# Graph attention and two-expert routing on one core: narrower rows for the first list, centred gate logits from raw rows, and a new order of the steps around them

## The reference

```python
# x: 64 x 128 x 128 (graphs g, nodes n, features d), adj: 64 x 128 x 128 of 0/1
h = layernorm(x)                                  # no scale, no bias
Wh = h @ W.T;  e = leaky_relu(Wh@a1 [:,None] + Wh@a2 [None,:], 0.2)
x = x + softmax(where(adj > 0, e, -9e15)) @ Wh    # the attention layer
z = layernorm(x)
logits = z @ gate_w + gate_b                      # 16 experts
top 2 of softmax(logits), renormalised -> gates
x = x + sum over the 2 chosen e of gate_e * ((silu(z @ w1[e]) * (z @ w2[e])) @ w3[e])
```

## Time and profile before

| | us |
|---|---|
| median of 3 runs (518.23 to 519.63) | 519.61 |
| the profiled execution | 513.99 |
| its span, first to last instruction | 512.2 |
| PE busy / DVE busy | 393.6 / 250.7 |
| ACT busy / POOL busy | 224.2 / 257.1 |

### The profile page before, as it was taken

The page is one execution under the profiler, slowest core; times in us unless marked ns, Lnnn a source line. Parts: engine busy times, 40 slices in busy tenths (PEclk is TensorE's granted clock), DMA queues, the critical chain, the costliest instruction groups (busy, mean ns, idle before and its releaser), DMA issues.

```text
span 512.2 us, 11503 instructions
## 1 busy us (share of the span) xinstructions
PE 393.6 (77%) x2993; PEld 357.2 (70%) x2994; DVE 250.7 (49%) x978; ACT 224.2 (44%) x583; POOL 257.1 (50%) x284
## 2 busy tenths in 40 slices
PE   6889788867685867079988788852998887888890
PEld 3678677755564766079977788852998887888880
DVE  4788989865786453024433344340342523424250
ACT  2799576563574513024424344320443423525240
POOL 5222346775328666426554655561355554555554
PEclk9999999987887678569999999985899999999996
DMA  3544345646173356577666666424654664555500
GB/s 105 158 130 135 90 154 158 185 155 208 43 228 116 135 178 235 204 236 248 222 221 193 202 215 225 152 71 124 184 182 158 189 186 160 164 179 187 164 28 1
DMA packets 75547, 83.35 MB, mean 163 GB/s; under 512 B 10564, under 2 KB 60111, under 8 KB 75504
## 3 DMA queue, kind: packets, MB, share of 16 engines
q1 hardware_dynamic: 66032, 61.58, 39.7%
q0 software_dynamic: 9472, 21.26, 11.8%
HBM read 36.06 MB, written 28.94 MB: 127 GB/s over the span
## 4 chain that ended last, share of the span: by engine, by line
PE 47%; issue 18%; DVE 10%; SPq 7%; POOL 6%; DMA 4%; ACT 3%; another core or an unknown queue 2%; ACTq 1%; POOLq 0%; DVEq 0%
PE bank L499 26%; PE bank L512 11%; PE bank L371 5%; SPq L303 4%; POOL sorted_rows L1014 3%; POOL rstd L1005 2%; DMA shared<-in_adj_dram 2%; DVE prob L931 1%; DMA R<-sorted_rows 1%; DVE stats L688 1%; SPq L318 1%; DVE h L698 1%; DVE R L744 1%; PE bank L419 1%
## 5 line engine op out<-in xcount | busy, mean ns | idle before, releaser
L499 PE MATMUL bank<-xT,w_t 128*128 128x128 f32 x1280 | 181.9, 285 | 25.2 <-issue 16.4
L499 PEld LDWEIGHTS bank<-xT,w_t 128*128 128x128 f32 x1280 | 164.1, 199 | 30.1 <-issue 19.7
L632 ACT ACTIVATE hT<-bank 128x256 f32<-128x256 f32 x160 | 60.5, 384 | 171.2 <-PE bank L499 97.1
L931 DVE TENSOR_TENSOR prob<-hT,bank 128x256 f32<-128x256 f32 x160 | 67.2, 420 | 136.9 <-ACT hT L632 76.9
L1039 POOL DMA_INDIRECT out_dram<-R x80 | 78.3, 979 | 80.1 <-DVE R L940 51.1
L512 PE MATMUL bank<-W,prob 128*128 x640 | 102.5, 284 | 14.3 <-issue 10.0
L1039 POOL DMA_INDIRECT sorted_rows<-R x80 | 78.4, 980 | 69.5 <-DVE R L940 48.3
L512 PEld LDWEIGHTS bank<-W,prob 128*128 128x128 f32 x640 | 86.8, 196 | 19.5 <-issue 18.6
L940 DVE SCALAR_TENSOR_TENSOR R<-bank,R 128x128 f32<-128x128 f32 x160 | 55.1, 346 | 65.9 <-PE bank L512 56.5
L1014 POOL DMA_INDIRECT sorted_rows<-R,ROW x64 | 62.7, 979 | 29.5 <-issue 16.7
L371 PE MATMUL bank<-ident,R 128*128 128x128 f32 x224 | 39.1, 299 | 45.7 <-DMA R<-sorted_rows 26.5
(11 more groups left out here) (129 smaller groups left out, 382.4 us busy)
## 6 DMA issues: line engine op xcount, KB each, us to landing
R<-sorted_rows SPq DMA_DIRECT2D x160, 130.0 KB
w_t<-W SPq DMA_DIRECT2D x80, 256.0 KB
W<-in_L_ffn_w_dram SPq DMA_DIRECT2D x48, 128.0 KB
sorted_rows<-pad SPq DMA_DIRECT2D x34, 130.0 KB
R<-in_x_dram SPq DMA_DIRECT2D x16, 256.0 KB
shared<-in_adj_dram SPq DMA_DIRECT2D x16, 256.0 KB
sorted_rows<-R POOLq DMA_INDIRECT x80
out_dram<-R POOLq DMA_INDIRECT x80
```

The lines of the kernel that those rows point to most:

```text
L499: ins = nc.tensor.matmul(H[k][:, m * P:(m + 1) * P], w_t[:, par, k, m * P:(m + 1) * P], xT[:, par, k * P:(k + 1) * P], start=True, stop=True)
L632: nc.scalar.activation(sil[:, k, :], H[k][:, 0:HC * P], ACT.Silu).then_inc(silu_ready, 1)
L931: V.tensor_tensor(hidT[:, k, :], sil[:, k, :], H[k][:, HC * P:2 * HC * P], ALU.mult).then_inc(hid_ready, 1)
```

## The change

1. The row kept for list 0 is 128 raw values of x2, two row numbers, two gates, mean and inverse root: 134 floats, 536 bytes. The normalised values aren't stored in it. DVE normalises a quad's rows once they are loaded (`normalize_rows`), two tiles after each of the first two `gate_hidden` of the quad before. Rows of list 1 keep 1,040 bytes and their normalised half. The row slots are a buffer of their own.
2. Gate logits are computed from raw x2: PE turns x2, multiplies by a centred `gate_w` (`centre` is the identity minus 1/128), DVE multiplies by the inverse root and then adds the bias. ACT's second normalisation goes, and so does round 20: step 4 is now part of step 3, and every later step of a batch is one round earlier.
3. ACT normalises two graphs of each group for the attention (`BY_ACT`), DVE the other two.
4. DVE, PE and ACT have new orders in a round (DVE: first aggregate and epsilon ahead of the x2 sum; PE: turn of x2 first, gate logits and attention behind the turn of h).
5. Experts: rows are turned after the third `up` of a quad (`TURN`), in both lists; quad 3 is finished before the rows of quad 4 are turned; the 16 padding blocks of list 1 stand behind the rows and weights of quads 6 and 7 (eight each); PE does 30 bf16 matmuls of 512 columns between the lists (`SWITCH`).

```diff
-    ROW2, DEST, GATE = 2 * D, 2 * D + 1, 2 * D + 2
+    ROW2, DEST, GATE = D, D + 1, D + 2
+    MEAN = GATE + NL
+    RSTD = MEAN + 1
+    WIDTH = (RSTD + 1, D + MEAN)
...
-        rows = R[:, 0:RB * QT, :]
+        rows = sb("rows", [P, RB * QT, D + RSTD + 1])
...
-            for i in range(NI + 4):
-                steps = {k: 0 <= i - k < NI for k in range(-1, 5)}
+            for i in range(NI + 3):
+                steps = {k: 0 <= i - k < NI for k in range(-1, 4)}
...
+        def early(c, q, behind):
+            return c == 0 and isinstance(q, int) and q == NQA + behind
+        def carried(row, c):
+            return row[:, D:D + WIDTH[0]] if c == 0 else row[:, 0:WIDTH[1]]
...
             load_up(3, 1)
-            for b in range(NE // QT):
-                clear_pads(1, b * QT, pad_in[1])
...
             for q in (RB, RB + 1):
                 load_quad(0, q, q - RB, 1)
                 load_up(q, q % 2)
+                for b in range(NE // QT // 2):
+                    clear_pads(1, ((q - RB) * (NE // QT // 2) + b) * QT, pad_in[1])
...
+                if has(3):
+                    pe.wait_ge(x2_ready, k + 1)
+                    turn(TH2, lambda g: R[:, k * GG + g, 0:D], x2_turned)
                 if has(2):
                     turn(TP, lambda g: prob[:, par, g * N:(g + 1) * N], prob_turned)
+                if chosen is not None:
+                    count(chosen)
+                if has(0):
+                    turn(TH, lambda g: h[:, par, g * D:(g + 1) * D], h_turned)
+                if has(3):
+                    for g in range(GG):
+                        ins = nc.tensor.matmul(LO[:, g * NE:(g + 1) * NE], x2T[:, g * N:(g + 1) * N], gw_c[:],
+                                               start=True, stop=True)
                 if has(2):
                     for g in range(GG):
                         ins = nc.tensor.matmul(HP[:, g * D:(g + 1) * D], probT[:, g * N:(g + 1) * N],
                                                Wh[:, par, g * D:(g + 1) * D], start=True, stop=True)
...
+                if c == 0:
+                    pe.wait_ge(h2_ready, q * QT + QT)
+                else:
+                    pe.wait_ge(xs_in[slot], (nth + uses(slot) + 1) * (16 * QT))
...
+                if c:
+                    pe.wait_ge(xT_ready, NQ)
+                    keep_warm(SWITCH, XP)
...
-                        if k == 0 and not last:
+                        if k == TURN and not last and not early(c, q, -1):
                             turn_rows(c, q + 1, (at + 1) % RB, nth + (at + 1) // RB)
...
-                    if last:
+                    if last or early(c, q, -1):
                         for k in range(QT - LAG, QT):
                             down(c, q, at, k, e[k])
+                    if early(c, q, -1):
+                        turn_rows(c, q + 1, (at + 1) % RB, nth + (at + 1) // RB)
...
+                for g in range(BY_ACT):
+                    nc.scalar.activation(h[:, par, g * D:(g + 1) * D], R[:, i * GG + g, 0:D], ACT.Identity,
+                                         bias=shift[:, par, g:g + 1], scale=rstd[:, par, g:g + 1])
...
+                    V.tensor_tensor(logits, LO[:, 0:GG * NE].rearrange("p (g e) -> p g e", e=NE),
+                                    R[:, k * GG:(k + 1) * GG, RSTD:RSTD + 1].broadcast_to([P, GG, NE]),
+                                    ALU.mult).then_inc(logits_scaled, 1)
...
+            def normalize_rows(q, at, nth, tiles):
+                slot = at % RB
+                dve.wait_ge(xs_in[slot], (nth + 1) * (16 * QT))
+                for k in tiles:
+                    r = rows[:, slot * QT + k, :]
+                    V.tensor_scalar(r[:, 0:D], r[:, D:2 * D], r[:, D + MEAN:D + MEAN + 1], r[:, D + RSTD:D + RSTD + 1],
+                                    ALU.subtract, ALU.mult).then_inc(h2_ready, 1)
...
+                        if c == 0 and k < 2 and not last and not early(c, q, -1):
+                            normalize_rows(q + 1, at + 1, nth + (at + 1) // RB, range(2 * k, 2 * k + 2))
...
-            DISPATCHED = {8: 4, 9: 4, 10: 4, 11: 6, 12: 6, 13: 5, 14: 3, 15: 3, 16: 4}
+            DISPATCHED = {7: 4, 8: 4, 9: 4, 10: 6, 11: 6, 12: 5, 13: 3, 14: 3, 15: 5, 16: 3}
```

More of the change, by code:

```diff
@@ L60, in gat_moe_kernel @@
     NOWHERE = 2 * XROWS
-    xs = [nc.dram_tensor(f"sorted_rows{c}", (XROWS, DW), F32, kind="Internal").ap() for c in range(NL)]
+    xs = [nc.dram_tensor(f"sorted_rows{c}", (XROWS, WIDTH[c]), F32, kind="Internal").ap() for c in range(NL)]
     ctx = ExitStack()
@@ L358, in _, with keep_warm @@
             pe.wait_ge(const_steps, 7)
-            for _ in range(WARM):
-                nc.tensor.matmul(RT[:], ones_bf[:], ones_bf[:, 0:1].broadcast_to([P, GG * N]), start=True, stop=True)
+            def keep_warm(n, into):
+                for _ in range(n):
+                    nc.tensor.matmul(into[:], ones_bf[:], ones_bf[:, 0:1].broadcast_to([P, GG * N]), start=True, stop=True)
+            keep_warm(WARM, RT)
             pe.wait_ge(small_in, 80)
-            pe.wait_ge(const_steps, 12)
+            pe.wait_ge(const_steps, 13)
             pe.wait_ge(setup_v, 1)
@@ L431, in iteration @@
                 if i == 0:
[L432 removed]
+                    nc.tensor.matmul(RT[:], ident[:], x2T[:], start=True, stop=True)
             def choose(b):
@@ L553, in iteration @@
                     nc.scalar.activation(probT[:], TP[:], ACT.Copy).then_inc(probT_ready, 1)
-                if has(3):
-                    k = i - 3
-                    act.wait_ge(shift_ready, k + 1)
-                    for g in range(GG):
-                        row = R[:, bass.ds(k * GG + g, 1), :].rearrange("p a d -> p (a d)")
-                        ins = nc.scalar.activation(row[:, 0:D], row[:, D:2 * D], ACT.Identity,
-                                                   bias=shift[:, 1 - par, g:g + 1],
-                                                   scale=rstd[:, 1 - par, GG + g:GG + g + 1])
-                    ins.then_inc(h2_ready, 1)
                 if chosen is not None:
@@ L657, in quad @@
                         silu(q * QT + (c * NT + k), k)
-                        if k == 0 and not last:
+                        if k == (QT - 1 if early(c, q, -1) else TURN) and not last:
                             copy_rows(c, q + 1, 1 - par)
@@ L950, in quad @@
                                     table=q if c == 0 and isinstance(q, int) and q in (1, 2) and k == LAG else None)
-                        elif not first:
+                        elif not first and not early(c, q, 0):
                             add_row(c, t + (k - LAG), at + RB - 1, k + (QT - LAG))
```

243 lines of the change are left out of this document (136 added, 107 removed).

## The result

The changed kernel took 534.38 us (median of 6 runs, 527.12 to 537.89) where the kernel before took 519.62 on the same chip: a ratio of 1.025, 95% interval 1.019 to 1.031. It is slower, and 34 us over the forecast.

A forecast was written before the change was run, and what follows sets the result against it. PE, ACT and DVE nearly fill the attention stage, PE bounds the lists, with a 59.6 us hole between. Terms -27 (to quad 4), +5, +7, 0, -3.5, and -1 for the dispatch, give -19.5 from 519.61: 500 us, range 494 to 507.

The forecast's parts named there:

- A: Attention rounds: DVE loses 0.33 us a round, PE's work unchanged; 15 rounds give -5 us, bounds 0 and -8.
- B: End of the attention stage: one round less before the last choice, -4 us, bounds -1 and -7.
- PE holds it: Attention rounds: one case for the bound of 0, in which PE keeps the round from getting shorter.
- C: From last choice to quad 4: -18 us; first tile of quad 4 near 201 instead of 228.18.
- C's two bounds: List 0's 16 padding blocks before quad 4: 16.5 us if issue sets the pace, 8.5 if bytes do.
- E: List 0: PE's turn waits 0.6 us a quad for DVE's normalisation; +7 us, bounds 0 and 12.
- D: List 0: list 1's padding behind quads 6 and 7 uses up SP's lead; +5 us, bounds 0 and +12.
- rival 3: List 0: VectorE becomes its pace, PE waiting 1.9 us a quad; +5 us in all, or 525; chance 0.11.
- F: List 0: narrower rows load fewer bytes, which were not its bound; 0 us, bounds -5 and 0.
- G: Switch between lists: 30 matmuls keep PE's clock up for list 1's first tiles; -3.5 us, bounds -4 and 0.
- Rival 4: List 0: DVE's normalisations block POOL's sends, up to 0.28 us each; +2 us at most, 502; chance 0.05.
- The turn later in the quad costs list 1 nothing: List 1: turn and copy take about 1.3 us, and 1.8 us of other PE work stands between; 0 us.

The follow-up runs named there:

- e6: Changed kernel, with logits and attention ahead of count and turn of h in rounds with a choice only: 522.45 us against the kernel before's 521.93 (0.999).
- e12: Changed kernel, with attention first in choice rounds, three tiles normalised early and one late: 451.11 us, 1.009 of the kernel before.
- e16: Changed kernel, with attention first in choice rounds, three tiles normalised early, list 1's padding four blocks at a time: 446.62 us against the kernel before's 446.68 (1.000).
- e2: Changed kernel, with only the count moved behind attention times Wh: 465.13 us against the kernel before's 446.14 (1.040).
- e10: Kernel before, with list 1's 16 padding blocks moved behind quads 6 and 7, eight each: ratio 1.006.
- e11: Kernel before, with list 1's padding behind quads 6 and 7 and quad 3 finished before quad 4's turn: ratio 1.002.
- e13: Changed kernel unaltered, timed in a 446 session: 470.79 us against the kernel before's 446.68 (1.055).
- e9: Kernel before unaltered, as a control against itself in a 446 session: ratio 1.000.
- e3: Kernel before, with list 1's 16 padding blocks moved behind quads 6 and 7: 448.58 us against 446.14 (1.003).
- e14: Kernel before, with list 1's padding four blocks at a time behind quads 6, 8, 10 and 12: 443.03 us against 446.68 (0.992).
- e18: Kernel before, with list 1's padding four blocks at a time, in a 520 session: 502.65 us against 514.3 (0.981).
- e5: Changed kernel unaltered, timed again in a 520 session: 532.92 us against the kernel before's 521.93 (1.018).
- e8: Changed kernel, with list 1's rows turned after the first up of a quad, as before: 532.5 us against the kernel before's 521.93 (1.016).
- e17: Changed kernel without the burst of thirty matmuls between the lists: 531.24 us against the kernel before's 514.3 (1.034).
- e4: Kernel before, with list 1's padding behind quads 6 and 7 and quad 3 finished first: 448.52 us against 446.14 (1.003).

## Why the prediction was wrong

**Steps A and B (forecast -9, measured +9.9, in a 446 session +10.0): this is the step that failed.** A said that "PE's work is unchanged" and counted instructions and their durations. It did not walk PE's new order against DVE's, although the change lists it: `count` and the turn of h ahead of attention put the end of DVE's choice, through PE, in front of DVE's own next input. The sum had no term for it. e6 undoes this in five rounds and takes 14 us off the last choice, e12 and e16 10 in the 446 sessions; that is shown. The order therefore cost 14 and 10 us, and all the rest of A and B brought about -4 and 0. In ordinary rounds A gave nothing: 6.85 us against 6.74. It took the round from DVE, whose work shrank, but PE held it: of 6.84 us PE is busy for 6.26, as it was for some 6.37 before, and the other 0.58 is its wait for ACT's two normalisations, as it was 0.25 to 0.47 for ACT's second normalisation (L559) before. That is A's own bound of 0, "PE holds it", through a wait that part 3 of the change put there. B (-4) was right where the idle pieces are few: from the last `hT,dst_w` matmul to the last choice the kernel before needs 24.2 us, the changed one in a 446 session 19.5, e2 and e12 18 to 19. In the 520 sessions the changed kernel needed 23.5 and 23.9. In the 446 sessions the rounds before take this gain back: e12 reaches its last `hT,dst_w` matmul at 143.6 us, the kernel before at 138.1.

**Step C (-18, with A and B quad 4's product at about 202.6; measured 240.94).** It failed too: the stage from choice to quad 4 changed by +1.3 us in the first session and by -3.6 in the 446 sessions. The mechanism is there: the wait for the rows of quad 4 shrinks, in e10 by 6 us, and e11's stage is 12.6 us shorter. Three things went otherwise. Its start was 19 us late by A and B. The padding of list 0 took 15.81 us, against 16.51 before, and 9.90 (e13) against 10.21 (e9) in the 446 sessions: of C's two bounds the one by issue came, not the one by bytes. And E acts in quads 1 to 3 already, where C had nothing for it: in e13 the stage takes 45.1 us, in e11, which has C's edits alone, 36.2, and PE's waits for normalised rows in that stage of e13 are 9.1.

**Step D (+5, range 0 to +12).** With eight blocks at a time, list 0 lost 8.5 to 9.8 us in e3 and e10, and 12.4 to 12.7 with quad 3 first, as the change has it: about twice the forecast, and at the end of its range. The reason given (SP's lead of two quads used up by the second eight) is what the trace of e10 shows. At four at a time it measured 4.8 in a 446 session (e14) and nothing in a 520 session (e18).

**Step E (+7, range 0 to 12).** In list 0 from quad 4 it measured 5.5 (e13 against e11) to 8.4 (e13 against e10), and most turns waited 0.4 to 0.6 us where E had 0.6: right in size and mechanism. With three tiles normalised early e12's list 0 is back at 102.4, between e10 and e11. Before quad 4 E cost about 9 more, which no step had. Together with D and C this answers rival 3, which decides from 1.6 us a quad: the waits were 19.4 us over 19 turns, 1.0 a turn, so VectorE's order did not become the pace of list 0. The sign of the result was that of rival 3, its mechanism was another, which stood among no rivals.

**Steps F and G.** F (0) stands, though a quad's loads shrink by 0.26 MB (512 rows of 504 bytes), not by 0.27: no run shows anything that list 0's rows at 536 bytes brought, and none has them alone. G (-3.5) measured -1.1 in the first session and +0.1 in a 446 session (16.8 in e13 against 16.7 in e9): mis-sized, with its own bound 0, that the clock falls again before the rows land, nearest to what came. Rival 4, the port rule: 80 normalisations of 373 ns beside the sends left these at 983 ns, against 980. By the rule of the Trainium skill ("SBUF — State Buffer", "Who interferes with whom") each could have taken up to 0.28 us more. The trace shows none of it for this instruction on these operands.

**List 1 (forecast 0, measured +7.9, in the 446 sessions -0.2).** "The turn later in the quad costs list 1 nothing" holds in the 446 sessions. In a 520 session (e5) 18.5 us of PE's waits in 15 pieces follow late copies; e8 gets 2.7 us of the stage back and e17, which keeps the late turn, shows 142.4. The cause of the +7.9 stays open: a part may be the late turn, the rest is of the size by which these profiles differ.

**The sum in a 446 session**, e13 against the kernel before in e9 (span 468.8 against 444.4): last choice +10.0, choice to quad 4 -3.6, list 0 +18.2, switch, list 1 and tail -0.1, together some 24.5. The forecast was -19.5. Of the 44 us between the two, A and B hold 19, C 14, D and E 6 and G nearly 4. With the order of PE right in rounds with a choice, three tiles normalised early and the padding spread, the median is that of the kernel before, and 3.6 us above e14, which has the spread padding alone; 3.0 of these are in list 0 (99.1 against 96.1). So of the parts tried alone only the moved padding gains in these sessions, and only when it is cut smaller. Narrow rows, logits from raw rows and ACT's share of the normalisation were not run alone.

**What stays open.** What the idle pieces of the 520 sessions are: no view names what releases them. Fetching of code, which the expectations of e3 and e4 have as a rival, was not tested; the instruction queues moved the same 18 and 25 packets in both kinds of session. That the pieces are not the kernel's own is shown by the same kernel nearly lacking them in other sessions; whether they belong to the chip or to the time isn't. Why e18 gained some 10 us (1.9%) there and e14 3.7 here was not tried further; part may be these pieces.

## What to carry to other kernels

When an order changes, walk every engine's new order against the others in each kind of round, the rare ones too: a wait for a long job of another engine, put ahead of that engine's own next input, costs both of them, and here the clock besides (10 to 14 us in five rounds). A window of the profile is read only after the rounds in it are known to be of one kind. Work moved off a critical wait into a queue with little slack has to be cut into pieces smaller than that slack: eight blocks at a time gave the whole gain back, four left 0.8% in one session and 1.9% in another. Time the kernel before in more than one session before believing the size of a hole.

## What the runs showed of the hardware

The same kernel took 446 us in some sessions and 514 to 522 us in others, at mean granted clocks of 0.917 and 0.910 in the two profiles. In the longer ones ACT stands for up to 7.7 us at a time with no releaser on the core (64.1 us in 16 such waits at one line), and others wait behind it: at 405.75 us of the kernel before ACT had stood for 5.82 us and DVE for 4.69, while PE had three waits of 0.6 to 1.1. In the kernel before they come from 106 us to the end. The label alone proves nothing: e2, in a 446 session, has 28.7 us of it on ACT, in 9 waits at a line that waits for PE in e13 (25.7 in 16). The longest seen was 11.4 us on DVE, in e6, and POOL's queue went on sending in it until 182.75:

```profile
174.21 0.96 POOL L1109 DMA_INDIRECT sorted_rows<-R,ROW  x1 [0.40 <-DVE R L897]
...
185.34 0.18 DVE L971 CAST PADS<-bank 1x32 int32<-1x32 f32 x1 [11.40 <-remote]
```

A DMA issue on SP also took longer there: the 16 padding blocks of list 0 took 13.5 to 15.8 us in three 520 sessions and 9.90 in a 446 session, in the changed kernel.
